# Two score tables of a two-block Swin kernel added up by VectorE inside its first two rounds, instead of by GpSimd and VectorE ahead of them

## The chip, the cores and the metric

The kernel runs on one core of one Trainium2 chip. The metric is the device time of one execution in microseconds (us); the median over repeated runs counts. The engines are TensorE (PE, with its weight loads as PEld), VectorE (DVE), ScalarE (ACT), GpSimd (POOL) and SyncE (SP). TensorE's clock has two levels, 1.2 and 2.4 GHz; the profile gives the granted clock as a share of the higher.

## The reference

Two Swin transformer blocks follow one another on x of shape (32, 56, 56, 96), in float32. Block 0 has 4 heads and a third layer norm inside its MLP, block 1 has 12 heads. In each block the image is shifted by 3 and cut into windows of 7 by 7 tokens:

```
h = roll(layer_norm(x), (-3, -3)) as windows of 49 tokens
q, k, v = h @ qkv_w + qkv_b
attn = softmax(q * scale @ k.T + rel_bias + attn_mask)
x = x + roll(attn @ v @ proj_w + proj_b, (3, 3))
m = gelu(layer_norm(x) @ fc1_w + fc1_b)      # block 0: then layer_norm(m)
x = x + m @ fc2_w + fc2_b
```

rel_bias is a table of relative positions that is the same for all windows; attn_mask is 0 or -100 and differs only between windows at the image's edge and the others. The sum of the two is a constant, in two forms: one for strips in the last row of windows and one for all others.

## The kernel before

The 32 images are cut into 256 strips of 8 windows (4 pairs of 98 tokens). A strip passes through a pipeline by hand: round i of the loop works on strip i (statistics of its first layer norm), strip i-1 (transposes), strip i-2 (attention of block 0), strip i-3 (its MLP), strip i-4 and i-5 (attention of block 1) and strip i-6 (its MLP, and the store). Each engine has its own `body(i)`, a list in fixed order of such steps; `iterate` writes out the first 9 rounds, loops over most of the rest and writes out the last ones. In rounds in which a strip doesn't exist the step is left out, so round 0 of VectorE is empty (the statistics of strip 0 were taken ahead), and round 1 holds two steps for it: `low_part_qk` of strip 0 and the statistics of strip 1. Engines wait for each other by semaphores that count upward.

The score of a window is not a matmul alone. Before the q k products are added up in a PSUM bank, ScalarE writes the sum of rel_bias and attn_mask there (`seed`, line 688, which reads the SBUF tensor `table`). The bank is then added to by TensorE (line 471). The first seeds are those of strip 0 in round 2.

`table` is 128 x 6272 in float32, two halves of 3136 columns: half 0 for ordinary strips, half 1 for the strips of the last row, of which the first is strip 224. ScalarE's DMA queue loads `t_in` (rel_bias; it is laid over the tensor `shifted`) and then the two masks into the halves of `table` (lines 619 and 621), three DMAs of 1568 KB each, and behind them, once VectorE has made them, two rows of biases into `wqkv` (line 624, 1.3 and 1.2 KB, semaphore `s_brow`). t_in is then added to each half:

- GpSimd adds half 0 as soon as t_in and mask 0 have landed (line 993).
- VectorE adds half 1 (line 982) at the end of its preparation, after the statistics of strip 0 (lines 846 to 854), and waits for GpSimd's half before its rounds begin.
- ScalarE waits for both (through `s_w` at 27 and `s_table`) before its first round, and so before its first table load (line 633).

VectorE's preparation is one chain in which every step waits for the one before: weights are scaled by the layer norms' gains (lines 810 to 815), split into a high and a low part (817 and 818 for the MLP; 831 and 832 for q and k, which wait for `s_brow` at 32), and the constant rows written (834). TensorE waits for `s_w` at 26 and for `s_brow` and then writes 6 of the 8 PSUM banks full once (line 401, 12 instructions). Its last instruction lets ScalarE go on (`s_wps` at 5), which then loads its function tables in turn: Gelu before that wait, then Exp, then Gelu (line 633). In round 1 GpSimd's normalised strip 0 (`rstdA` line 1000, `xnA` lines 1007 and 1011) is transposed by TensorE (line 407), and ScalarE reads the transpose out (`xqT_high` line 646, `xnT` line 647), after which TensorE makes v (line 450), k and q (422, 423, 425). SyncE's queue then spreads k over the heads (`kM`, line 342), and TensorE multiplies (line 471).

The code around the additions before:

```
            stats(Strip(0, 0), "A0", ahead=True)
            dve.wait_ge(s_tables[0], 32)
            dve.wait_ge(s_tables[1], 16)
            done(dve.tensor_tensor(table[:, NT:2 * NT], table[:, NT:2 * NT], t_in, ALU.add))
            dve.wait_ge(s_table, 1)
            iterate(dve, body)
```

Of the kernel before, what the change touches and what calls it, by code (L numbers as in the profile page):

```python
# [81 lines left out]
def swin_program(nc, d, out, ns=NSTRIP, last_row_from=NSTRIP - NSTRIP // ROWS_IN_IMAGE):  # L82
    f32, f32r = mybir.dt.float32, mybir.dt.float32r
    ALU, ACT, AX = mybir.AluOpType, mybir.ActivationFunctionType, mybir.AxisListType
    ctx = ExitStack()
    with ctx:
# [18 lines left out]
        NT = UNIT_COLS * NUNIT  # L105
        table = sb("table", [128, 2 * NT])
# [69 lines left out]
        s_tables = [sem(f"s_tables{v}") for v in (0, 1)]  # L176
# [77 lines left out]
        def bank_free(x, use):  # L254

            at = [n for n, _, _ in BANKS].index(use)
            own, wraps = BANKS[at][1], 0
            for _ in range(4 * len(BANKS)):
                at -= 1
                if at < 0:  # L260
                    at, wraps = at + len(BANKS), wraps + 1
                other, lag, bank = BANKS[at]
                y = Strip(x.i, x.off + lag + wraps - own)
                if bank == bank_of[use] and y.exists(ns):
                    semaphore, per, c = over[other]
                    return semaphore, y.count(per, c)
            return None
# [8 lines left out]
                      (rows[L][:, :], d[f"rows{L}"]), (wproj[L][:, :], d[f"wproj{L}"])]  # L276
        NCONST = 16 * len(loads)

        NMEMSET, NW_BROW, NW = 13 + len(O_BANKS), 4, 27

        def iterate(eng, body):

# [89 lines left out]
        def _(pe):  # L372
# [20 lines left out]
                          start=(c == 0), stop=False)  # L393
            pe.matmul(ps[5][0:PT, 0:C], ones[0:1, 0:PT], rows[0][0:1, W3[0]:W3[0] + C], start=False, stop=True)
            pe.matmul(ps[6][0:PT, 0:C], ones[0:1, 0:PT], rows[1][0:1, W3[1]:W3[1] + C], start=True, stop=True).then_inc(s_wps, 1)
            pe.wait_ge(s_w, NW - 1)
            pe.wait_ge(s_brow, 32)
            for n in range(8):
                if n in O_BANKS:
# [216 lines left out]
        def _(act):  # L616
# [7 lines left out]
                act.dma_start(wqkv[L][C:C + 1, :], brow[L][0:1, :]).then_inc(s_brow, 16)  # L624
            act.wait_ge(s_wps, 5)
            act.wait_ge(s_w, NW)
            act.wait_ge(s_table, 1)

            def table_ahead(x, n):

# [52 lines left out]
            def seed(x, L, u):  # L683

                if x.exists(ns):
                    if free_from := bank_free(x, f"sc{L}{u}"):
                        act.wait_ge(*free_from)
                    act.activation(ps[bank_of[f"sc{L}{u}"]][0:SP, 0:UNIT_COLS], table_of(x, L, u), ACT.Copy).then_inc(s_sd[L], 1)  # L688
# [84 lines left out]
        def _(dve):  # L773
# [16 lines left out]
            def done(ins, wait=True):  # L790
                step[0] += 1
                ins.then_inc(s_w, 1)
                if wait:
                    dve.wait_ge(s_w, step[0])
# [80 lines left out]
            def shift(x, L, u):  # L875
                if not x.exists(ns):
                    return
                dve.wait_ge(s_s[L], x.count(UNITS[L], u + 1))
                buf = unit_buffer(L, u)
                s = ps[bank_of[f"sc{L}{u}"]][0:SP, 0:UNIT_COLS].rearrange("p (h k) -> p h k", k=TOK)  # L880
                dve.tensor_reduce(negmax[:, buf, :], s, AX.X, ALU.max, negate=True).then_inc(s_mx[L], 1)  # L881
                if x.back().exists(ns):
                    dve.wait_ge(s_ex[L], x.back().count(UNITS[L], u + 1))
                dve.wait_ge(s_mx[L], x.count(UNITS[L], u + 1))
                dve.tensor_tensor(shifted[0:SP, buf, :].rearrange("p (h k) -> p h k", k=TOK), s,  # L885
                                  free(negmax[:, buf, 0:1], (1, 8), (0, TOK)), ALU.add).then_inc(s_sh[L], 1)
# [49 lines left out]
            def finish0(x):  # L936
# [11 lines left out]
                                                   op0=ALU.mult, op1=ALU.add)  # L948
                ins.then_inc(s_fin[0], 1)

            def body(i):
                s0, s1, s2, s3, s4, s5, s6 = Strip(i, 0), Strip(i, 1), Strip(i, 2), Strip(i, 3), Strip(i, 4), Strip(i, 5), Strip(i, 6)
                shift(s5, 1, 3)
                finish0(s4)
                normalise(s3, 0)
                stats(s4, "A1")
                shift(s5, 1, 4)
                shift(s5, 1, 5)
                residual(s3, 0)
                stats(s3, "M0")  # L960
                low_part(s6, 1)
                shift(s2, 0, 0)
                low_part_qk(s4, 1)
                shift(s2, 0, 1)
                normalise(s5, 1)
                low_part_qk(s1, 0)
                low_part(s3, 0)
                stats(s0, "A0")
                residual(s5, 1)
                stats(s5, "M1")  # L970
                finish1(s6)
                shift(s4, 1, 0)
                shift(s4, 1, 1)
                shift(s4, 1, 2)
                third_stats(s3)
# [1 line left out]


            stats(Strip(0, 0), "A0", ahead=True)
            dve.wait_ge(s_tables[0], 32)  # L980
            dve.wait_ge(s_tables[1], 16)
            done(dve.tensor_tensor(table[:, NT:2 * NT], table[:, NT:2 * NT], t_in, ALU.add))  # L982
            dve.wait_ge(s_table, 1)
            assert step[0] == NW
            iterate(dve, body)

        @block.gpsimd
        def _(pool):
            for L in (0, 1):
                pool.memset(kM[L][:, :, :], 0.0).then_inc(s_memset, 1)  # L990
                pool.memset(vM[L][:, :, :, :, :], 0.0).then_inc(s_memset, 1)
            pool.wait_ge(s_tables[0], 32)
            pool.tensor_tensor(table[:, 0:NT], table[:, 0:NT], t_in, ALU.add).then_inc(s_table, 1)

            def inverse_root(x, n):
                if x.exists(ns):
                    pool.wait_ge(s_var[n], x.count(1, 1))
                    if x.back().exists(ns):
                        pool.wait_ge(s_xn[n], x.back().count(1, 1))
                    pool.tensor_tensor(rstd[n][:, :], var_eps[n][:, :], minus_half[:, :], ALU.pow).then_inc(s_rstd[n], 1)  # L1000

            def norm(x, n):
                if not x.exists(ns):
                    return
                if x.back().exists(ns):
                    pool.wait_ge(s_xt[n], x.back().count(1, 1))
                pool.tensor_tensor(xn[n][:, :, :], SRC[n][:, :, :], free(mv[n][:, 0, 0:1], (2, PAIRS), (0, C)),
                                   ALU.subtract).then_inc(s_xc[n], 1)
                pool.wait_ge(s_xc[n], x.count(1, 1))
                pool.wait_ge(s_rstd[n], x.count(1, 1))  # L1010
                pool.tensor_tensor(xn[n][:, :, :], xn[n][:, :, :], free(rstd[n][:, 0:1], (1, PAIRS), (0, C)),
                                   ALU.mult).then_inc(s_xn[n], 1)

            def add_bias(x, L):
                if x.exists(ns):
                    pool.wait_ge(s_xo[L], x.count(1, 1))
                    if x.back().exists(ns):
                        pool.wait_ge(s_fin[L], x.back().count(1, 1))
                    pool.tensor_tensor(x_biased[L][:, :, :], x_mid[L][:, :, :], free(bfc2[L][:, 0:1], (0, PAIRS), (1, C)), ALU.add)\
                        .then_inc(s_xb[L], 1)  # L1020

            def squares(x):
                if not x.exists(ns):
                    return
                pool.wait_ge(s_ge[0], x.count(HCH, HCH))
                if x.back().exists(ns):
                    pool.wait_ge(s_f2[0], x.back().count(1, 1))
                pool.tensor_tensor(hid_sq[:, :, :], hid[0][:, :, :], hid[0][:, :, :], ALU.mult).then_inc(s_sq, 1)  # L1028
                pool.wait_ge(s_sq, x.count(3, 1))
                pool.tensor_tensor(hid_ss[:, :], hid_sq[:, 0, :], hid_sq[:, 1, :], ALU.add).then_inc(s_sq, 1)  # L1030
                pool.wait_ge(s_sq, x.count(3, 2))
                pool.tensor_tensor(hid_ss[:, :], hid_ss[:, :], hid_sq[:, 2, :], ALU.add).then_inc(s_sq, 1)

            def rstd_of_third(x):
                if x.exists(ns):
                    pool.wait_ge(s_v3, x.count(4, 4))
                    if x.back().exists(ns):
                        pool.wait_ge(s_fin[0], x.back().count(1, 1))
                    pool.tensor_tensor(rstd3[:, :], var3[:, :], minus_half[:, :], ALU.pow).then_inc(s_rstd3, 1)

            def body(i):
                s0, s3, s4, s5 = Strip(i, 0), Strip(i, 3), Strip(i, 4), Strip(i, 5)
                inverse_root(s4, "A1")
                norm(s4, "A1")
                inverse_root(s3, "M0")
                norm(s3, "M0")
                inverse_root(s0, "A0")
                add_bias(s3, 0)
                squares(s3)
                norm(s0, "A0")  # L1050
                inverse_root(s5, "M1")
                rstd_of_third(s3)
                norm(s5, "M1")
                add_bias(s5, 1)

            iterate(pool, body)
# [88 lines left out]
```

## Time and profile before

| | |
|---|---|
| median of 3 runs | 6497.58 us (6496.65 to 6502.27) |
| span of the profiled execution | 6496.8 us, 0.8 us under that median; no other time is given for it |
| TensorE busy | 6430.3 us (99%) |
| ScalarE busy | 5702.6 us (88%) |
| VectorE busy | 5350.0 us (82%) |
| GpSimd busy | 4516.1 us (70%) |
| granted TensorE clock, mean | 0.993 |

The span is the time from the first to the last instruction. "Busy" is the time in which an engine had an instruction under way, whether it computed or was held up in it. Because one strip passes per round, a few us at the beginning or the end stand once in the total, and a change in a round stands some 250 times in it.

### The profile page before, as it was taken

Reading aid. Unit: us, or ns where it says so; the run is one execution under the profiler, and the core shown is the slowest. Engines: PE = TensorE matmul, PEld = TensorE weight load, DVE = VectorE, ACT = ScalarE, POOL = GpSimd, SP = SyncE. Lnnn points to the kernel's source line nnn. Section 1 sums busy time; section 2 is a strip of 40 time slices with the busy share of each in tenths; the row PEclk is TensorE's granted clock in tenths of the full one; section 3 lists DMA queues with packets and bytes.
Section 4 is the critical chain, followed back from the end, with each engine's and each line's share of the span. In section 5 each row is a group of like instructions: output and inputs, shape, how many; then the busy total and the mean of one; then the engine's idle time right before and its main releaser. Section 6 shows DMA issues by size and latency. Waiting matters only on the chain.

```text
span 6496.8 us, 288677 instructions
## 1 busy us (share of the span) xinstructions
PE 6430.3 (99%) x97836; PEld 5929.2 (91%) x97836; DVE 5350.0 (82%) x19240; ACT 5702.6 (88%) x12312; POOL 4516.1 (70%) x4617
## 2 busy tenths in 40 slices
PE   6999999999999999999999999999999999999999
PEld 5999999999999999999999999999999999999998
DVE  5888888888888888888888888888888888888886
ACT  5888888888888888888888888888888888888887
POOL 4676767676767676777777777767676767676764
PEclk8999999999999999999999999999999999999998
DMA  2111111111111111111111111111111111111111
GB/s 68 51 51 50 51 50 51 50 50 50 51 50 51 50 52 49 52 49 51 50 50 50 50 51 50 51 50 51 49 51 50 51 50 51 50 50 50 51 50 36
DMA packets 604534, 327.88 MB, mean 50 GB/s; under 512 B 449916, under 2 KB 603902, under 8 KB 604094
## 3 DMA queue, kind: packets, MB, share of 16 engines
q1 hardware_dynamic: 603992, 322.32, 18.9%
q10 hardware_dynamic: 486, 4.82, 0.2%
q8 instruction: 35, 0.57, 0.0%
q14 instruction: 21, 0.17, 0.0%
HBM read 82.89 MB, written 38.54 MB: 19 GB/s over the span
## 4 chain that ended last, share of the span: by engine, by line
PE 98%; DVE 1%; issue 0%; ACT 0%; POOL 0%; DMA 0%; SPq 0%; DVEq 0%; ACTq 0%; POOLq 0%
PE ps L407 22%; PE ps L558 17%; PE ps L504 13%; PE ps L471 10%; PE ps L422 8%; PE ps L425 7%; PE ps L423 7%; PE ps L450 6%; PE ps L528 6%; PE ps L565 2%; PE ps L401 0%; DVE wfc_high L817 0%; DVE negmax L881 0%; DMA kM<-kT 0%; DMA wproj<-in_wproj 0%
## 5 line engine op out<-in xcount | busy, mean ns | idle before, releaser
L1000 POOL TENSOR_TENSOR rstdA<-var_epsA,minus_half 98x4 f32<-98x4 f32 x512 | 521.3, 1018 | 1348.7 <-DVE var_epsA L854 1348.6
L885 DVE TENSOR_TENSOR shifted<-ps,negmax 113x392 f32<-113x392 f32 x2048 | 1160.6, 567 | 241.7 <-DVE negmax L881 54.6
L881 DVE TENSOR_REDUCE negmax<-ps 113x8 f32<-113x392 f32 x2048 | 1144.6, 559 | 218.0 <-PE ps L471 217.9
L703 ACT ACTIVATE probsT<-ps 98x392 f32<-98x392 f32 x2048 | 959.4, 494 | 343.4 <-PE ps L407 342.8
L696 ACT ACTIVATE probs<-shifted 113x392 f32<-113x392 f32 x2048 | 1044.6, 522 | 125.2 <-DVE shifted L885 124.5
L407 PE MATMUL ps<-ident,probs 113*98 113x113 f32 x8192 | 1076.2, 264 | 9.5 <-ACT probs L696 8.1
L688 ACT ACTIVATE ps<-table 113x392 f32 (+1 forms) x2048 | 941.5, 499 | 28.4 <-DVE x_mid L908 2.4
L504 PEld LDWEIGHTS ps<-vM,probsT 98*49 98x49 f32 x32768 | 816.7, 125 | 137.7 <-issue 73.8
L504 PE MATMUL ps<-vM,probsT 98*49 98x18 f32 (+1 forms) x32768 | 899.6, 202 | 0.1
L407 PEld LDWEIGHTS ps<-ident,probs 113*98 113x98 f32 x8192 | 823.9, 130 | 47.9 <-ACT probs L696 12.5
L720 ACT ACTIVATE hid<-ps,bfc 128x392 f32<-128x392 f32 x1536 | 786.0, 586 | 14.8 <-PE ps L425 8.8
L1000 POOL TENSOR_TENSOR rstdM<-var_epsM,minus_half 98x4 f32<-98x4 f32 x512 | 518.2, 1012 | 386.5 <-DVE var_epsM L854 386.5
L633 ACT ACT_TABLE_LOAD x524 | 672.3, 1283 | 45.9 <-DVE table L982 36.8
L471 PE MATMUL ps<-kM,qT 32*49 32x196 f32 (+1 forms) x20480 | 688.1, 299 | 14.1 <-ACT ps L688 7.3
L558 PE MATMUL ps<-wfc,hid 128*98 128x97 f32 x6144 | 665.7, 255 | 0.0
L558 PEld LDWEIGHTS ps<-wfc,hid 128*98 128x98 f32 x6144 | 599.6, 168 | 0.0
L558 PE MATMUL ps<-par,hid 128*98 128x96 f32 (+1 forms) x6144 | 579.5, 251 | 0.7 <-ACT hid L720 0.7
L422 PE MATMUL ps<-xnT_high,wfc_high 96*128 96x392 f32 x1536 | 575.4, 375 | 2.9 <-DVE xnT_low L872 1.3
L471 PEld LDWEIGHTS ps<-kM,qT 32*49 32x49 f32 (+1 forms) x20480 | 438.5, 118 | 140.9 <-issue 98.1
L1028 POOL TENSOR_TENSOR hid_sq<-hid 128x1176 f32<-128x1176 f32 x256 | 549.1, 2145 | 14.8 <-ACT hid L720 14.8
L558 PEld LDWEIGHTS ps<-par,hid 128*98 128x98 f32 x6144 | 557.1, 168 | 1.2 <-ACT hid L720 1.2
L423 PE MATMUL ps<-xnT_high,wfc_low 96*128 96x392 f32 x1536 | 527.0, 343 | 0.0
(105 smaller groups left out, 15058.1 us busy)
## 6 DMA issues: line engine op xcount, KB each, us to landing
kM<-kT SPq DMA_DIRECT2D x512, 85.8 KB
vM<-vA SPq DMA_DIRECT2D x1024, 41.3 KB
vM<-vA SPq DMA_DIRECT2D x1024, 38.3 KB
x_in<-in_x SPq DMA_DIRECT2D x256, 147.0 KB
x_again<-in_x SPq DMA_DIRECT2D x256, 147.0 KB
kM<-kT SPq DMA_DIRECT2D x1024, 36.8 KB
x_keep<-x_next SPq DMA_DIRECT2D x256, 147.0 KB
out_y<-y_out SPq DMA_DIRECT2D x256, 147.0 KB
```

Of the source, the lines that this page charges most:

```text
L407: return pe.matmul(out, x, ident[0:rows, 0:rows], start=first, stop=last, is_transpose=True, skip_group_check=True)
L422: pe.matmul(out, w_high, x_high, start=True, stop=False)
L423: pe.matmul(out, w_low, x_high, start=False, stop=False)
L471: mm = pe.matmul(ps[bank_of[f"sc{L}{u}"]][HALF[h]:HALF[h] + TOK, n * p:n * (p + 1)], qT[L][r, t:t + TOK], kM[L][r, :, t:t + TOK], start=Fa ...
L504: mm = pe.matmul(g[HALF[h]:HALF[h] + TOK, col:col + width], probsT[:, unit_buffer(L, u), p * heads // 2 + n, h, :], vM[L][:, 2 * (first + ...
L558: mm = pe.matmul(g[0:PT, p * step:p * step + width], hid[L][:, c, t], w, start=(p == c == 0), stop=(c == HCH - 1), skip_group_check=True)
L688: act.activation(ps[bank_of[f"sc{L}{u}"]][0:SP, 0:UNIT_COLS], table_of(x, L, u), ACT.Copy).then_inc(s_sd[L], 1)
L696: act.activation(probs[:, buf, :], shifted[0:SP, buf, :], ACT.Exp).then_inc(s_ex[L], 1)
L703: act.activation(probsT[:, unit_buffer(L, u), :, :, :], free(ps[bank_of[f"T{L}{u}"]][0:PT, 0:1], (SP, 4), (64, 2), (1, TOK)), ACT.Copy).th ...
L881: dve.tensor_reduce(negmax[:, buf, :], s, AX.X, ALU.max, negate=True).then_inc(s_mx[L], 1)
L885: dve.tensor_tensor(shifted[0:SP, buf, :].rearrange("p (h k) -> p h k", k=TOK), s, free(negmax[:, buf, 0:1], (1, 8), (0, TOK)), ALU.add).t ...
L1000: pool.tensor_tensor(rstd[n][:, :], var_eps[n][:, :], minus_half[:, :], ALU.pow).then_inc(s_rstd[n], 1)
```

## The change

Both halves are now added by VectorE, in its `body`: half 0 as the first thing of round 0 and half 1 as the first thing of round 1 (`add_table`). GpSimd's addition is gone, as is VectorE's wait for it. ScalarE's wait for `s_table` before its first round is gone, and `s_w` ends at 26; a wait for `s_table` at 2 stands before each seed of strip 0 instead.

```
--- before.py
+++ after.py
@@ -276,7 +276,7 @@
                       (rows[L][:, :], d[f"rows{L}"]), (wproj[L][:, :], d[f"wproj{L}"])]
         NCONST = 16 * len(loads)
 
-        NMEMSET, NW_BROW, NW = 13 + len(O_BANKS), 4, 27
+        NMEMSET, NW_BROW, NW = 13 + len(O_BANKS), 4, 26
 
         def iterate(eng, body):
 
@@ -393,7 +393,7 @@
                           start=(c == 0), stop=False)
             pe.matmul(ps[5][0:PT, 0:C], ones[0:1, 0:PT], rows[0][0:1, W3[0]:W3[0] + C], start=False, stop=True)
             pe.matmul(ps[6][0:PT, 0:C], ones[0:1, 0:PT], rows[1][0:1, W3[1]:W3[1] + C], start=True, stop=True).then_inc(s_wps, 1)
-            pe.wait_ge(s_w, NW - 1)
+            pe.wait_ge(s_w, NW)
             pe.wait_ge(s_brow, 32)
             for n in range(8):
                 if n in O_BANKS:
@@ -624,7 +624,6 @@
                 act.dma_start(wqkv[L][C:C + 1, :], brow[L][0:1, :]).then_inc(s_brow, 16)
             act.wait_ge(s_wps, 5)
             act.wait_ge(s_w, NW)
-            act.wait_ge(s_table, 1)
 
             def table_ahead(x, n):
 
@@ -683,6 +682,8 @@
             def seed(x, L, u):
 
                 if x.exists(ns):
+                    if x.known and x.i == x.off:
+                        act.wait_ge(s_table, 2)
                     if free_from := bank_free(x, f"sc{L}{u}"):
                         act.wait_ge(*free_from)
                     act.activation(ps[bank_of[f"sc{L}{u}"]][0:SP, 0:UNIT_COLS], table_of(x, L, u), ACT.Copy).then_inc(s_sd[L], 1)
@@ -948,8 +949,16 @@
                                                    op0=ALU.mult, op1=ALU.add)
                 ins.then_inc(s_fin[0], 1)
 
+            def add_table(x, v):
+
+                if x.known and x.i == v:
+                    dve.wait_ge(s_tables[v], 32 - 16 * v)
+                    dve.tensor_tensor(table[:, v * NT:(v + 1) * NT], table[:, v * NT:(v + 1) * NT], t_in, ALU.add).then_inc(s_table, 1)
+
             def body(i):
                 s0, s1, s2, s3, s4, s5, s6 = Strip(i, 0), Strip(i, 1), Strip(i, 2), Strip(i, 3), Strip(i, 4), Strip(i, 5), Strip(i, 6)
+                add_table(s0, 0)
+                add_table(s0, 1)
                 shift(s5, 1, 3)
                 finish0(s4)
                 normalise(s3, 0)
@@ -977,10 +986,6 @@
 
 
             stats(Strip(0, 0), "A0", ahead=True)
-            dve.wait_ge(s_tables[0], 32)
-            dve.wait_ge(s_tables[1], 16)
-            done(dve.tensor_tensor(table[:, NT:2 * NT], table[:, NT:2 * NT], t_in, ALU.add))
-            dve.wait_ge(s_table, 1)
             assert step[0] == NW
             iterate(dve, body)
 
@@ -989,8 +994,6 @@
             for L in (0, 1):
                 pool.memset(kM[L][:, :, :], 0.0).then_inc(s_memset, 1)
                 pool.memset(vM[L][:, :, :, :, :], 0.0).then_inc(s_memset, 1)
-            pool.wait_ge(s_tables[0], 32)
-            pool.tensor_tensor(table[:, 0:NT], table[:, 0:NT], t_in, ALU.add).then_inc(s_table, 1)
 
             def inverse_root(x, n):
                 if x.exists(ns):
```

On VectorE, where its preparation ends and its rounds begin, before (`table<-table,shifted` is the addition of t_in to one half; `xqT_low` is the first step of round 1):

```order
L854 TENSOR_SCALAR var_epsA<-mvA 98x4 [waits s_bnA0]
L982 TENSOR_TENSOR table<-table,shifted 128x3136 [waits s_tables1,s_tables0]
L864 TENSOR_TENSOR xqT_low<-ps,xqT_high 96x392 [waits s_xeA0,s_table,s_w]
L846 BN_STATS bnA<-x_in 98x6 [waits s_xnA0,s_load]
L846 BN_STATS bnA<-x_in 98x6 x3
```

and with the change:

```order
L855 TENSOR_SCALAR var_epsA<-mvA 98x4 [waits s_bnA0]
L956 TENSOR_TENSOR table<-table,shifted 128x3136 [waits s_tables0]
L956 TENSOR_TENSOR table<-table,shifted 128x3136 [waits s_tables1]
L865 TENSOR_TENSOR xqT_low<-ps,xqT_high 96x392 [waits s_xeA0]
L847 BN_STATS bnA<-x_in 98x6 [waits s_xnA0,s_load]
L847 BN_STATS bnA<-x_in 98x6 x3
```

The two additions stand next to one another, since round 0 holds nothing else for VectorE, and ahead of the first step of round 1.

On GpSimd, from its last memset to its first strip, before:

```order
L991 MEMSET vM 98x864
L993 ISA
L993 TENSOR_TENSOR table<-table,shifted 128x3136 [waits s_tables0]
L1000 TENSOR_TENSOR rstdA<-var_epsA,minus_half 98x4 [waits s_varA0]
L1007 TENSOR_TENSOR xnA<-x_in,mvA 98x384
```

and with the change:

```order
L996 MEMSET vM 98x864
L1003 ISA
L1003 TENSOR_TENSOR rstdA<-var_epsA,minus_half 98x4 [waits s_varA0]
L1010 TENSOR_TENSOR xnA<-x_in,mvA 98x384
```

The addition is gone, and GpSimd's first arithmetic is that of strip 0. TensorE's and SyncE's instructions and waits are the same in both kernels; on ScalarE only the waits differ, at the first table load and at the eight seeds of strip 0.

## Rows read from the trace of the kernel before

**Rows 1.** The page, busy time of the engines and the chain by line.
```profile
PE 6430.3 (99%) x97836; PEld 5929.2 (91%) x97836; DVE 5350.0 (82%) x19240; ACT 5702.6 (88%) x12312; POOL 4516.1 (70%) x4617
...
PE 98%; DVE 1%; issue 0%; ACT 0%; POOL 0%; DMA 0%; SPq 0%; DVEq 0%; ACTq 0%; POOLq 0%
```

**Rows 2.** Groups by line, TensorE, 200 to 6400 us: count | busy, mean ns | idle before.
```profile
L471 PE MATMUL ps<-kM,qT 32*49 32x196 f32 (+1 forms) x19920 | 667.3, 298 | 3.9 <-ACT ps L688 0.2 <-DMA kM<-kT 0.2
```

**Rows 3.** The chain that ended last, 0 to 50 us: start, duration, what.
```profile
21.66 6.83 DVE wfc_high L817
...
32.03 7.34 PE ps L401 x12
...
42.42 0.20 ACT spark_gelu L633
```

**Rows 4.** Timeline, 0 to 60 us: start, duration, engine, line, operation [idle before].
```profile
20.68 0.35 DVE L817 CAST wfc_high<-wfc 96x384 fp32r<-96x384 f32 x1
...
21.43 6.83 POOL L993 TENSOR_TENSOR table<-table,shifted 128x3136 f32<-128x3136 f32 x1 [17.13 <-DMA table<-in_mask]
21.66 6.82 DVE L817 CAST wfc_high<-wfc 96x384 fp32r<-96x384 f32 x1
...
29.81 0.27 DVE L831 CAST wqk_high<-wqkv 97x224 fp32r<-97x224 f32 x1
```

**Rows 5.** Timeline, 0 to 40 us, ScalarE's DMA queue: start, duration of the issue.
```profile
16.97 2.16 ACTq L624 DMA_DIRECT2D wqkv<-brow  x2
```

**Rows 6.** The tile table, 0 to 60 us: mask DMAs, their first and last start, landing.
```profile
L621 ACTq DMA_DIRECT2D table<-in_mask x2: 450/452/453, 11.5 to 12.0; - x2
...
DMA to landing us min/median/max: 9.9/11.5/13.2
```

**Rows 7.** Windows: busy by engine, clock, DMA share, GB/s last.
```profile
24.00:24.50 0.50, 0.00 (x0) 0.00 (x0) 0.50 (x1) 0.00 (x0) 0.50 (x1) 1.00 0.20 55
24.50:25.00 0.50, 0.00 (x0) 0.00 (x0) 0.50 (x1) 0.00 (x0) 0.50 (x1) 1.00 0.01 1
```

**Rows 8.** Timeline, 32 to 60 us: strip 0 on its way to the first scores.
```profile
33.28 3.43 DVE L982 TENSOR_TENSOR table<-table,shifted 128x3136 f32<-128x3136 f32 x1
33.45 4.14 POOL L1000 TENSOR_TENSOR rstdA<-var_epsA,minus_half 98x4 f32<-98x4 f32 x1 [5.19 <-DVE var_epsA L854]
...
38.47 0.83 POOL L1011 TENSOR_TENSOR xnA<-xnA,rstdA 98x384 f32<-98x384 f32 x1
...
39.35 0.54 PE L407 MATMUL ps<-ident,xnA 98*96 98x98 f32 x4
...
42.53 0.47 ACT L646 ACTIVATE xqT_high<-ps 96x392 fp32r<-96x392 f32 x1
...
43.43 1.20 PE L450 MATMUL ps<-wqkv,xnT 97*98 97x100 f32 x8 [3.54 <-ACT xnT L647]
...
45.42 1.01 POOL L1000 TENSOR_TENSOR rstdA<-var_epsA,minus_half 98x4 f32<-98x4 f32 x1 [6.12 <-DVE var_epsA L854]
...
47.04 0.91 ACT L688 ACTIVATE ps<-table 113x392 f32<-113x392 f32 x2
...
49.53 1.56 PE L471 MATMUL ps<-kM,qT 48*49 48x98 f32 x32 [2.92 <-DMA kM<-kT]
...
59.24 1.65 PE L450 MATMUL ps<-wqkv,xnT 97*98 97x100 f32 x8
```

**Rows 9.** Windows in the filling of the pipeline: PE busy first, clock third from the end.
```profile
42.00:44.00 2.00, 0.57 (x6) 0.57 (x7) 0.49 (x2) 1.97 (x5) 0.00 (x0) 0.99 0.00 0
44.00:65.00 21.00, 13.94 (x113) 11.34 (x111) 6.10 (x29) 10.74 (x21) 5.26 (x6) 0.51 0.15 38
68.00:81.00 13.00, 8.21 (x37) 7.28 (x38) 3.90 (x16) 5.92 (x11) 9.12 (x9) 0.50 0.05 11
82.00:91.00 9.00, 6.18 (x88) 4.88 (x90) 5.40 (x31) 3.63 (x8) 4.25 (x5) 1.00 0.17 53
92.00:109.00 17.00, 13.43 (x78) 10.95 (x77) 7.68 (x23) 11.61 (x24) 8.79 (x9) 0.51 0.13 32
```

More of the change, by code:

```diff
@@ L277, in swin_program @@
         NCONST = 16 * len(loads)
-        NMEMSET, NW_BROW, NW = 13 + len(O_BANKS), 4, 27
+        NMEMSET, NW_BROW, NW = 13 + len(O_BANKS), 4, 26
         def iterate(eng, body):
@@ L395, in _ @@
             pe.matmul(ps[6][0:PT, 0:C], ones[0:1, 0:PT], rows[1][0:1, W3[1]:W3[1] + C], start=True, stop=True).then_inc(s_wps, 1)
-            pe.wait_ge(s_w, NW - 1)
+            pe.wait_ge(s_w, NW)
             pe.wait_ge(s_brow, 32)
@@ L626, in _ @@
             act.wait_ge(s_w, NW)
-            act.wait_ge(s_table, 1)
             def table_ahead(x, n):
@@ L685, in seed @@
                 if x.exists(ns):
+                    if x.known and x.i == x.off:
+                        act.wait_ge(s_table, 2)
                     if free_from := bank_free(x, f"sc{L}{u}"):
@@ L949, in finish0, with add_table @@
                 ins.then_inc(s_fin[0], 1)
+            def add_table(x, v):
+                if x.known and x.i == v:
+                    dve.wait_ge(s_tables[v], 32 - 16 * v)
+                    dve.tensor_tensor(table[:, v * NT:(v + 1) * NT], table[:, v * NT:(v + 1) * NT], t_in, ALU.add).then_inc(s_table, 1)
             def body(i):
                 s0, s1, s2, s3, s4, s5, s6 = Strip(i, 0), Strip(i, 1), Strip(i, 2), Strip(i, 3), Strip(i, 4), Strip(i, 5), Strip(i, 6)
+                add_table(s0, 0)
+                add_table(s0, 1)
                 shift(s5, 1, 3)
@@ L979, in _ @@
             stats(Strip(0, 0), "A0", ahead=True)
[L980 to L983, printed above, removed]
             assert step[0] == NW
@@ L991, in _ @@
                 pool.memset(vM[L][:, :, :, :, :], 0.0).then_inc(s_memset, 1)
-            pool.wait_ge(s_tables[0], 32)
-            pool.tensor_tensor(table[:, 0:NT], table[:, 0:NT], t_in, ALU.add).then_inc(s_table, 1)
             def inverse_root(x, n):
```

## The prediction

> **What bounds the kernel.** I read the page first: TensorE is busy for 99% of the span and holds 98% of the chain that ended last [rows 1]. The groups of TensorE's instructions between 200 and 6400 us, where the rounds are all alike, show that the only idle time before any of its matmuls is 3.9 us in all, at line 471 [rows 2]. A round there is TensorE's own work. The change touches nothing in those rounds and nothing in TensorE's list, so it can pay or cost only once, in the preparation and in the first rounds, ahead of about 110 us, the end of the last stretch at the lower clock [rows 9]. There I read the chain of waits for the order of causes, the timeline for what two engines did at the same moment, the tile table for the landing of its DMAs, and windows for the clock. About 0.2% of the time, 13.0 us, is what a measurement of this kernel can tell from no change; the whole preparation ends at some 40 us, so any gain has to be large in it to be seen.
>
> The chain of the first 50 us has one odd piece: VectorE's cast into `wfc_high`, 6.83 us long [rows 3]. The timeline has the same cast twice, with the same shape: 0.35 us for block 0, 6.82 us for block 1 [rows 4]. What differs is GpSimd: its addition to the table begins at 21.43 and ends at 28.26, the slow cast begins at 21.66 and ends at 28.48 [rows 4]. So the cast was held until 0.22 us after GpSimd's addition, and everything behind it on VectorE with it. Behind it lie the rest of the preparation, TensorE's 12 instructions of line 401 (32.03, 7.34 us), ScalarE's changes of table up to the last at 42.42 [rows 3], and strip 0.
>
> **What it removes.** The addition on GpSimd goes. The cast falls from 6.82 to the 0.35 us of its twin: **6.47 us** earlier on VectorE. The step after it that has a wait of its own is line 831, which started at 29.81 [rows 4] and would now be reached at 29.81 - 6.47 = 23.34.
>
> **What is late next.** Line 831 waits for the bias rows in `wqkv`. Before, it had no wait to show, so their landing is not in the trace and I bound it. They were issued from 16.97 to 19.13 [rows 5], on the queue that still carried the masks. The second mask was issued at 12.0 and took 13.2 us, so it landed at 25.2; the first landed at 11.5 + 9.9 = 21.4, which is when GpSimd began [rows 6]. The DMA engines moved 55 GB/s in 24.0 to 24.5 and 1 GB/s in 24.5 to 25.0 [rows 7], so the last of the small rows cannot have landed much before 24.6. From above only 29.81 bounds it, when VectorE passed. I take 25.2, the landing of the mask that moved next to it, as a copy behind 4.7 MB should come with or just after the last of these: that takes back 25.2 - 23.34 = **1.86 us**, leaving 4.61. The ends are 24.6 (0.6 us better) and about 27.0, two us after the last bytes (1.8 us worse).
>
> The Trainium skill ("DMA: Bandwidth & Descriptors", Queues, rings and completion order) says that completions are not in order per issuing engine, but that each DMA engine consumes its descriptors in ring order and its semaphore write comes after its earlier writes; by that the rows land about with the mask, never well before it, and an early 23.3 is out.
>
> **What it adds.** A second addition on VectorE: 3.43 us by the row of the first [rows 8]. VectorE itself has room. It was idle from 36.71, when its addition ended, until the transpose's low part, which waits for ScalarE's 42.53 [rows 8]. The seeds read `table` at 47.04 [rows 8], and the second half is done at 33.28 - 4.61 + 2 x 3.43 = 35.5, so ScalarE's new waits are free by over 7 us; if this cover went, each us of delay would stand once in the end. Both inputs have landed by then.
>
> Its cost lies on GpSimd. `rstdA` of strip 0 took 4.14 us where its twin of the next strip took 1.01, and it ended at 37.59, 0.88 us after VectorE's addition ended at 36.71 [rows 8]. So that addition held GpSimd. Now two stand back to back. Either `rstdA` waits for both, or it slips in between and the subtraction after it waits for the second; by both, `xnA` ends one addition later than it would: 39.30 - 4.61 + 3.43 = 38.12 (39.30 is the end of line 1011, 38.47 + 0.83 [rows 8]). TensorE's turn of it began at 39.35 and ended at 39.89, so it now ends at 38.71. ScalarE's changes of table are paced by line 401 alone and end 4.61 us earlier, ready for line 646 at 37.92 instead of 42.53. So ScalarE waits 38.72 - 37.92 = **0.80 us** for the turn: GpSimd's path, which had about 2.6 us of slack before, has become the longer one. Left: 3.81.
>
> The Trainium skill ("SBUF — State Buffer", Who interferes with whom) has a rule that speaks against this change: a VectorE operation with two inputs in SBUF locks out a GpSimd instruction that reads SBUF, whole instruction by whole instruction, and whoever came first holds the pair. The trace agrees (4.14 against 1.01 us). By the rule the sum keeps the 0.80; if the second addition held nobody, the sum would lose that term and be 0.8 us better.
>
> **The clock.** TensorE's granted clock was 0.99 of full in 42 to 44 us and 0.51 from 44 to 65 [rows 9], after it had stood idle for 3.54 us ahead of line 450 [rows 8]. In the changed kernel it is idle between line 401 and the turn as well, from 34.8 to 38.2, so I let the clock fall one step earlier: line 450's first group of 8, on the path, then takes the 1.65 us of the next strip's group at the lower clock instead of 1.20 [rows 8]: **0.45 us** back. Bounds: 0, and 0.8 if the turn is slow too.
>
> **Sum.** 6.47 - 1.86 - 0.80 - 0.45 = 3.36 us. Behind it, every step of the first rounds waits for another engine or for a DMA of its own round, so all move together. Taking away ScalarE's wait for the table is by itself worth nothing: the additions ended at 36.71, but line 401, which it waits for too, ended at 32.03 + 7.34 = 39.37 [rows 3, 8]. The span goes from 6496.8 to 6493.4. The runs' median stood 0.8 above that span; taken off the median the time is 6497.58 - 3.36 = **6494.2 us**.
>
> **Rivals.**
> 1. *Held less, landed earlier.* The bias rows are there at 23.3 and the second addition holds nobody: all 6.47 us arrive, 6491.1. For it: nothing shows their landing. Against: the queue's traffic up to 24.5 and the 4.14 us. Chance 0.07.
> 2. *The cast was not held by GpSimd's addition* but by something that stays (the mask's DMA ran beside it too). Then nothing is won, and the second addition pushes `xnA` from 39.30 to 42.73, the turn's end to 43.32, and line 646 from 42.53 to 43.35: slower by 0.8 us, 6498.4. It decides once GpSimd's path is more than 2.6 us late. Against: the cast outlasted the DMA traffic by 4 us and ended with GpSimd's addition to 0.22 us. Chance 0.05.
> 3. *The clock in the filling.* From 44 to 109 us it was at the lower level for most of the time, with 9 us at full in 82 to 91 [rows 9]. The levels change with TensorE's pauses, and these shift. If the 6.18 us of matmuls in that full stretch ran at half, up to 6.2 us would be lost: 6500.4. If those of 68 to 81 (8.21 us at 0.50) ran at full, up to 4.1 would be won: 6490.1. Chance 0.08 for each of the two. That before's three runs lie 5.6 us apart agrees with such shifts.
> 4. *A round of the steady part changes its length*, through another phase between the engines. It needs 0.05 us in each of some 250 rounds to be 13 us, 6507 or more. TensorE's 3.9 us of idle time leave nothing to win there, and its list is the same, so I give 0.02 to slower, 0.01 to faster by over 13 us.
>
> **How the numbers follow.** The forecast, its three us, has 0.69; the rivals 0.07, 0.05, 0.16 and 0.03. The range goes from 6489.0 (below the faster clock, and rival 1 with a part of it) to 6500.0 (rival 2, and most of the slower clock); it takes in both ends of the landing. Same, within 13.0 us: 0.69 + 0.07 + 0.05 + 0.16 = 0.97, less 0.01 for clock shifts that add up: 0.96. Faster by more 0.015, slower by more 0.025.
>
> **What would show it.** In the changed profile: the second cast into `wfc_high` at 0.35 us; an idle stretch on VectorE ahead of line 832 (831 before) of about 1.9 us, that ends on a DMA near 25.2; line 401's group at about 27.4; two additions of 3.43 us; `rstdA` at 7 us or more, or a subtraction of 4; the turn of strip 0 at 38.2; ScalarE's `xqT_high` at 38.7; the first scores at 46.2 instead of 49.53 [rows 8]; rounds of the same length. A cast still at 6.8 us, or a `rstdA` at 1 us, would prove a step wrong. A time outside 6489 to 6500 would mean that something outside the first 110 us moved.

## The result, and the profile after

The changed kernel took 6478.17 us (median of 6 runs, 6473.17 to 6479.65), the kernel before 6497.66 us beside it (6 runs, 6494.0 to 6502.27). The ratio is 0.9966, with a 95% interval of 0.9956 to 0.9977: about 19.5 us faster. I had forecast 6494.2, which is 3.4 us faster, and a range of 6489.0 to 6500.0; to anything faster by more than 13 us I had given a chance of 0.015. The size was out by a factor of six.

The page of the changed kernel; its chain is TensorE's to the same 98% as in [rows 1]:

```profile
PE 6411.6 (99%) x97836; PEld 5920.2 (91%) x97836; DVE 5350.8 (83%) x19241; ACT 5701.7 (88%) x12312; POOL 4511.3 (70%) x4616
...
PE 98%; DVE 0%; POOL 0%; issue 0%; DMA 0%; ACT 0%; SPq 0%; DVEq 0%; ACTq 0%; POOLq 0%
```

The start came out as forecast. The timeline of the changed kernel, 20 to 60 us (start, duration, engine, line, operation, idle before):

```profile
20.55 0.36 DVE L818 CAST wfc_high<-wfc 96x384 fp32r<-96x384 f32 x1
...
21.53 0.36 DVE L818 CAST wfc_high<-wfc 96x384 fp32r<-96x384 f32 x1
...
25.24 0.28 DVE L832 CAST wqk_high<-wqkv 97x224 fp32r<-97x224 f32 x1 [1.94 <-DMA wqkv<-brow]
...
28.73 6.75 DVE L956 TENSOR_TENSOR table<-table,shifted 128x3136 f32<-128x3136 f32 x2
28.90 7.47 POOL L1003 TENSOR_TENSOR rstdA<-var_epsA,minus_half 98x4 f32<-98x4 f32 x1 [24.59 <-DVE var_epsA L855]
...
38.13 0.62 PE L407 MATMUL ps<-ident,xnA 98*96 98x98 f32 x4 [3.79 <-POOL xnA L1014]
38.78 0.49 ACT L645 ACTIVATE xqT_high<-ps 96x392 fp32r<-96x392 f32 x1 [1.18 <-PE ps L407]
...
39.72 1.65 PE L450 MATMUL ps<-wqkv,xnT 97*98 97x100 f32 x8 [0.97 <-ACT xnT L646]
...
46.27 1.56 PE L471 MATMUL ps<-kM,qT 48*49 48x98 f32 x32 [2.92 <-DMA kM<-kT]
```

Set against [rows 4] and [rows 8]: both casts take 0.36 us, VectorE then stands for 1.94 us until the bias rows land, `rstdA` is held for both additions, and the first scores start at 46.27 instead of 49.53, 3.26 us earlier. The rest does not come from here.

It comes from the rounds. VectorE's last step of a strip, `y_out`, 205 rounds apart; of before, then of after:

```profile
1002.50 0.54 DVE L917 TENSOR_TENSOR y_out<-x_biased,ps 98x384 f32<-98x384 f32 x1
...
6110.34 0.54 DVE L917 TENSOR_TENSOR y_out<-x_biased,ps 98x384 f32<-98x384 f32 x1
```

```profile
1022.79 0.54 DVE L918 TENSOR_TENSOR y_out<-x_biased,ps 98x384 f32<-98x384 f32 x1
...
6114.89 0.54 DVE L918 TENSOR_TENSOR y_out<-x_biased,ps 98x384 f32<-98x384 f32 x1
```

That is (6110.34 - 1002.50) / 205 = 24.916 us a round before and (6114.89 - 1022.79) / 205 = 24.839 after, 0.077 us less. By this instruction the two profiled executions differ as follows (strip 3 is the fourth to be finished, strip 249 the 250th):

| | before | after | difference |
|---|---|---|---|
| first scores start | 49.53 | 46.27 | -3.26 |
| from there to y_out of strip 3 | 180.61 | 181.78 | +1.17 |
| to y_out of strip 249, 246 rounds | 6129.43 | 6110.67 | -18.76 |
| to the end | 137.21 | 132.74 | -4.47 |
| sum (span) | 6496.78 | 6471.46 | -25.32 |

The filling and the end vary with TensorE's granted clock: the last part of the table was between 129.4 us (e1, mean granted clock 0.93 in that stretch) and 138.1 us (e10, 0.84) in the profiles of the kernels below; before it was 137.2 at 0.84, after 132.7 at 0.89. The profiled execution of the changed kernel (6473.27 us) was the second shortest of its six.

**Where in the round.** I laid a round of each over the other, from `y_out` at 3045.63 before and at 3034.74 after. Every instruction of every engine up to 12.2 us into the round stands at the same place to 0.015 us, but for three of VectorE that start 0.12 us earlier and move nobody else. Then ScalarE's seeds of block 0 (line 688 before, 689 after) start 0.09 us earlier, with them TensorE's scores of block 0 (0.07 to 0.08 us), and everything behind. Before:

```profile
3057.65 0.55 DVE L908 TENSOR_TENSOR x_mid<-x_again,ps 98x384 f32<-98x384 f32 x1
3057.84 0.53 ACT L696 ACTIVATE probs<-shifted 113x392 f32<-113x392 f32 x1 [0.23 <-DVE shifted L885]
...
3058.46 0.92 ACT L688 ACTIVATE ps<-table 113x392 f32 x2
...
3059.00 0.50 PE L407 MATMUL ps<-ident,xnA 98*96 98x98 f32 x4
...
3059.52 0.89 PE L471 MATMUL ps<-kM,qT 48*49 48x98 f32 x32
```

and after:

```profile
3046.75 0.54 DVE L909 TENSOR_TENSOR x_mid<-x_again,ps 98x384 f32<-98x384 f32 x1
3046.95 0.53 ACT L697 ACTIVATE probs<-shifted 113x392 f32<-113x392 f32 x1 [0.23 <-DVE shifted L886]
...
3047.48 0.92 ACT L689 ACTIVATE ps<-table 113x392 f32 x2
...
3048.10 0.50 PE L407 MATMUL ps<-ident,xnA 98*96 98x98 f32 x4
...
3048.55 0.89 PE L471 MATMUL ps<-kM,qT 48*49 48x98 f32 x32
```

From the start of `x_mid` to that of the seeds it is 0.81 us before and 0.73 after; from the turn (line 407) to the scores 0.52 and 0.45. The turn lasts 0.50 in both, so before the scores hardly wait by the profile (0.02 us), and after they overlap the turn's end by 0.05: together the 0.07 us. (The ends of matmuls in the profile are modelled, so how the 0.07 splits up rests on that model; the starts don't.)

The trace also holds ScalarE's register and semaphore instructions, which the views leave out. Between `x_mid` and the seed stands one register operation, which works out the seed's column in `table` and carries the wait for the bank that `x_mid` frees. From its start to the seed's start:

```
                  median   min     max    (245 rounds)
before            0.232    0.231   0.241
after             0.153    0.153   0.154
```

In the changed kernel a gap of 0.09 us stands 7 instructions earlier instead, behind an exponential (0.103 against 0.014 us to the next record). And the waits that the change put at strip 0's seeds have made ScalarE's list ahead of the loop 7 instructions longer (417 in place of 410; `s_table` once less, eight times more). Waits are instructions of the list where they don't fit on the one behind them; one semaphore instruction carries up to two (in e8 below 80 waits make the list 40 longer). The loop itself is the same 109 instructions. VectorE has such a gap too, of 0.12 us. Its list ahead of the loop is one instruction shorter, and the gap moved from ahead of one instruction to behind it; e2 below has it at the new place as well, and the long rounds.

### The profile page after: what moved, and what is told of

Same layout as the page of the kernel before. It is cut to its first block, busy times and chain, and to the rows that moved or that the text cites. A ratio compares the mean times of both kernels' runs of the same rounds, so it can differ in the third digit from the quotient of the medians.

```text
span 6471.5 us, 288682 instructions
## 1 busy us (share of the span) xinstructions
PE 6411.6 (99%) x97836; PEld 5920.2 (91%) x97836; DVE 5350.8 (83%) x19241; ACT 5701.7 (88%) x12312; POOL 4511.3 (70%) x4616
## 4 chain that ended last, share of the span: by engine, by line
PE 98%; DVE 0%; POOL 0%; issue 0%; DMA 0%; ACT 0%; SPq 0%; DVEq 0%; ACTq 0%; POOLq 0%
PE ps L407 22%; PE ps L558 17%; PE ps L504 13%; PE ps L471 10%; PE ps L422 8%; PE ps L425 7%; PE ps L423 7%; PE ps L450 6%; PE ps L528 6%; PE ps L565 2%; POOL rstdA L1003 0%; DMA wqkv<-brow 0%; DMA kM<-kT 0%; DMA wproj<-in_wproj 0%; DVE negmax L882 0%
## 5 line engine op out<-in xcount | busy, mean ns | idle before, releaser
L697 ACT ACTIVATE probs<-shifted 113x392 f32<-113x392 f32 x2048 | 1044.5, 522 | 126.8 <-DVE shifted L886 126.7
L425 PE MATMUL ps<-xnT_low,wfc_high 96*128 96x392 f32 x1536 | 526.6, 343 | 0.0
```

The source lines that it names most:

```text
L425: return pe.matmul(out, w_high, x_low, start=False, stop=True)
L697: act.activation(probs[:, buf, :], shifted[0:SP, buf, :], ACT.Exp).then_inc(s_ex[L], 1)
```

## The experiments

Three theories were open at first. A: a gap of about 0.08 us lies at a fixed place of ScalarE's list, so in each round of the loop ahead of whatever instruction sits there, and the change moved it off the seed. B: the earlier start put the engines into another phase. C: the list of VectorE or GpSimd decides, not ScalarE's. All kernels below were timed in turns with the kernel before, and each difference is to its median beside them.

**Waits alone (e1).** The kernel before, with the eight waits and nothing else:

```
-            act.wait_ge(s_table, 1)            # ahead of ScalarE's rounds
+                    if x.known and x.i == x.off:
+                        act.wait_ge(s_table, 1)    # in seed()
```

> The kernel before with one thing changed: ScalarE waits for the table (s_table at 1) at each of the eight seeds of strip 0 instead of once ahead of its rounds. No addition is moved. Its list ahead of the loop grows by 7 instructions, as in the change. Theory A (the place in ScalarE's list decides: a gap of about 0.08 us in its issue falls once per round at a fixed place of the list, in the kernel before right on the first seed of block 0): rounds of 24.84 us instead of 24.916, and no gain at the start, so 6497.7 - 245 x 0.077 = 6479, give or take 4. Theory B (the earlier start brings the engines into another, better phase): rounds stay at 24.916 and the time at 6497.7, since the start is not earlier. Theory C (GpSimd's or VectorE's list decides): also 6497.7.

6476.67 us against 6498.42, ratio 0.9965 (0.9951 to 0.998). The first scores start at 49.26, as in before, so nothing is won at the start; the register operation is 0.153 us ahead of the seed, the round 24.833 us (on ScalarE, from one return of the loop to the next). Waits that are met long before bring the whole gain of the change: 21.8 us here, against 19.5 and, with e7 below, 19.3 for the change.

**The change with the list as long as before (e2).**

```
-                    if x.known and x.i == x.off:
-                        act.wait_ge(s_table, 2)    # in seed()
+                    if L == 0 and x.known and x.i == x.off:
+                        act.wait_ge(s_table, 2)    # ahead of the copy xnT, in turned()
```

> The changed kernel with one wait for the table instead of eight, at ScalarE's copy xnT of strip 0 (line 646), an instruction that had no wait. VectorE's and GpSimd's lists are those of the change, both additions as there; ScalarE's list ahead of the loop is as long as before (410 in place of 417). Theory A: the first scores still at 46.3 us, rounds of 24.916 us again, 6497.7 - 3.4 = 6494.3, which is what I had forecast for the change. Theory B and C: rounds of 24.84 and the changed kernel's 6478.

6495.68 against 6498.42, ratio 0.9994 (0.9985 to 1.0004): 2.7 us less, within what the measurement can tell from nothing. The first scores start at 46.27 and the round is 24.918 us, the register operation 0.232 us ahead of the seed. B falls with these two kernels: one has the early start and the long round, the other the late start and the short round. Theory C, that VectorE's or GpSimd's list decides, falls as well: these are not what differs, since they are those of the change in e2 and those of before in e1. The windows 1000 to 1200 us of e1, then of e2 (length, busy of PE, PEld, DVE, ACT, POOL, clock, DMA share, GB/s):

```profile
1000.00:1200.00 200.00, 200.00 (x3073) 185.23 (x3072) 167.96 (x603) 178.25 (x386) 142.18 (x146) 1.00 0.20 51
```

```profile
1000.00:1200.00 200.00, 199.88 (x3065) 184.84 (x3064) 167.15 (x602) 177.86 (x385) 141.42 (x146) 1.00 0.19 50
```

**The gap moved in small steps (e3, e4, e9, e10).** Each is the kernel before with ScalarE's list ahead of the loop longer by 1, 3 and 2 instructions, or shorter by 1:

```
             act.wait_ge(s_table, 1)
+            for _ in range(2):                 # e3; 5 in e4, 3 in e9
+                act.wait_ge(s_table, 1)
```

```
-                        act.wait_ge(s_k[L], x.back().count(1, 1))      # e10, in turned()
+                        if not x.known or x.i > 2:
+                            act.wait_ge(s_k[L], x.back().count(1, 1))
```

> The kernel before with ScalarE's list ahead of the loop one instruction longer (two more waits for the table, met already, behind the one that is there). Theory A: the gap falls one instruction earlier in the round, ahead of the register operations of the first seed (line 688). These sit directly ahead of it on the same engine, so the seed is late by the same 0.08 us: rounds of 24.91, 6497.7. B and C: 6497.7 as well; this run tells only with the next one.

> The kernel before with ScalarE's list ahead of the loop three instructions longer (five more waits for the table, met already). Theory A: the gap falls behind line 651 and ahead of the exponential's register operation, where ScalarE has to wait 0.6 us for VectorE in each round anyway: it is hidden, rounds of 24.84, 6479 give or take 4. B and C: 6497.7.

> The kernel before with ScalarE's list ahead of the loop two instructions longer (three more waits for the table, met already). The gap now falls directly ahead of the exponential (line 696), behind the register operation that waits 0.6 us for VectorE in each round. If the gap is a fetch that goes on while the sequencer waits, it is hidden there: rounds of 24.83, 21 us under before. If each gap delays the instruction behind it whatever the sequencer did, the exponential and the seed behind it are 0.08 us late: rounds of 24.91, no gain.

> The kernel before with ScalarE's list ahead of the loop one instruction shorter (in round 2 the wait for the k of the strip before is left out where the transpose is read; the wait for its q covers it, which TensorE makes later). The gap falls behind the first seed of block 0 instead of ahead of it, where ScalarE is still busy with that seed for 0.4 us. If only the place between the seed's register operation and the seed costs: rounds of 24.83 and 21 us under before. If the second seed's place costs as well: rounds of 24.9.

| kernel | list ahead of the loop | the gap shows up | round, us | median, us | before beside it | ratio (95%) |
|---|---|---|---|---|---|---|
| before | 410 | between register operation and seed, 0.079 | 24.916 | | | |
| e10 | 409 | behind the seed, 0.081 | 24.833 | 6475.72 | 6493.49 | 0.9975 (0.9965 to 0.9985) |
| e3 | 411 | nowhere | 24.833 | 6475.47 | 6498.42 | 0.9964 (0.995 to 0.9978) |
| e9 | 412 | ahead of the exponential, 0.078 | 24.834 | 6475.96 | 6493.49 | 0.9974 (0.9964 to 0.9983) |
| e4 | 413 | nowhere | 24.833 | 6475.75 | 6498.42 | 0.9965 (0.9951 to 0.9979) |
| e1 | 417 | 7 earlier | 24.833 | 6476.67 | 6498.42 | 0.9965 (0.9951 to 0.998) |

Of all these places one costs. e3 was a miss of mine: I had taken ScalarE's own work for what the seed waits for, so that a gap ahead of the register operation should cost the same. It does not, because the register operation waits for `x_mid` in each round, and the gap passes in that wait; e4's lies in another wait. In these two the gap itself can't be seen, only that the seed's 0.079 us are gone. In e9 the gap is not hidden, as half of what I wrote there supposed: the exponential does start 0.078 us later; but the register operation behind it still starts on `x_mid`, and the seed with it.

**One more instruction ahead of the seed (e6).**

```
+                    if not x.known and (L, u) == (0, 0):
+                        act.wait_ge(s_w, NW)
+                        act.wait_ge(s_w, NW)
                     act.activation(...)            # in seed()
```

> The changed kernel with one more semaphore instruction on ScalarE, met already, directly ahead of the first seed of block 0 in every round of the loop. Theory A (the start of this seed sets TensorE's scores and with them the round): the sequencer reaches the seed 0.04 to 0.08 us later, and the round grows by as much: 24.88 to 24.91 us, 6487 to 6498. If the seed were not on the path: 24.84, 6478.

6472.47 against 6493.43, ratio 0.9971 (0.9959 to 0.9982), round 24.834 us: no cost, the same error as in e3. The instruction was placed ahead of the register operation, not between it and the seed as meant, and ran 0.025 us behind the exponential's start; the register operation followed 0.355 us later, when `x_mid` was ready.

**Blocks of 256 (e8, e11, e12).** The changed kernel with 40, 249 and 269 instructions more ahead of the loop, made of waits that are met already:

```
+            for _ in range(80):                # 498 in e11, 538 in e12
+                act.wait_ge(s_w, NW_BROW)
             act.wait_ge(s_wps, 5)
```

> The changed kernel with ScalarE's list ahead of the loop 40 instructions longer again (47 more than before; 80 waits that are met already, at a place where ScalarE waits for TensorE anyway). Theory A: the gap moves to a place some 11 instructions before the loop's first, so at the back end of the round, near the seeds of block 1 or the exponentials; unless one of these decides for TensorE, the round stays at 24.84, and the time at 6478. A round of 24.9 would mean that there is a second place that costs.

> The changed kernel with ScalarE's list ahead of the loop 249 instructions longer (498 waits that are met already): 256 more than before. If the gap comes wherever the list passes from one block of 256 instructions to the next, it is back ahead of the first seed of block 0: register operation to seed 0.232 us, rounds of 24.916 us, and the time within 6 us of before's (the waits themselves take 249 x 0.077 = 19.2 us of ScalarE's 15.2 us of idle time ahead of its first round, so the start is later by some 4 us). If the gap in before came from something else, such as the sum of waits ahead of the loop: 0.153 us, rounds of 24.83, 16 us under before.

> The same with 20 instructions more (276 more than before), as the control for the cost of so many waits. With blocks of 256 the gap falls 20 instructions earlier in the round than in the kernel before: register operation to seed 0.153 us, rounds of 24.83 to 24.84 us, about 18 us less than the kernel with 256, though it starts 1.5 us later.

| kernel | list | register operation to seed | round, us | median, us | before beside it | ratio (95%) |
|---|---|---|---|---|---|---|
| e8 | 457 | 0.153 | 24.834 | 6476.12 | 6493.43 | 0.9971 (0.9959 to 0.9982) |
| e11 | 666 = 410 + 256 | 0.253 | 24.939 | 6503.8 | 6499.89 | 1.0006 (0.9996 to 1.0016) |
| e12 | 686 | 0.153 | 24.837 | 6478.27 | 6499.89 | 0.9962 (0.9948 to 0.9977) |

The gap returns ahead of the same instruction when the list is 256 longer, and 20 instructions further it is gone from there again. The time of e11 also holds a later start (first scores at 51.06 us, in e12 at 52.36), since that many waits outlast ScalarE's idle time; the rounds are free of that. e12 carries more of the added waits than e11 and is still 25.5 us faster. e11's gap is 0.100 us (0.253 - 0.153) where before's is 0.079, and its rounds are 0.106 us longer than the short ones (24.833) where before's are 0.083: the round pays the gap in full. TensorE shows it in the windows, e11 first, e12 second:

```profile
1000.00:1200.00 200.00, 199.69 (x3061) 184.60 (x3060) 167.19 (x602) 178.16 (x387) 140.83 (x144) 1.00 0.19 50
```

```profile
1000.00:1200.00 200.00, 200.00 (x3067) 185.15 (x3066) 167.96 (x604) 178.92 (x389) 140.69 (x144) 1.00 0.19 50
```

e8 adds one thing: there the loop's return on ScalarE takes 0.155 us to the next record, in all the others of the first table 0.245 (0.255 in e11 and e12), and no gap is left inside the loop. I had expected the gap at the back end of the round; it left the loop. By the distance of 256 e8's 109 instructions lie in one block, those of the others in two. The slower return costs no time here: e8's rounds are as long as e3's or e10's, because ScalarE waits right behind it (1.72 us in the others, 1.81 in e8).

**Is it a refill by DMA in each round?** No. The DMA packets of before of the kind "instruction", in the whole execution:

```profile
q8 instruction: 35, 0.57, 0.0%
q14 instruction: 21, 0.17, 0.0%
```

and between 240 and 6300 us, where the loop runs, there is none in before and none in e11; these are all the queues of that stretch, before first:

```profile
q1 hardware_dynamic: 572872, 305.48, 19.2%
```

```profile
q1 hardware_dynamic: 572508, 305.00, 19.3%
```

So the gap comes in each round though nothing is fetched from outside. What ScalarE does in it the runs don't show.

**The second addition later (e5).** The changed kernel, with half 1 added at the end of round 1:

```
                 add_table(s0, 0)
-                add_table(s0, 1)
...
                 stats(s0, "A0")
+                add_table(s0, 1)
...
-                        act.wait_ge(s_table, 2)
+                        act.wait_ge(s_table, 1 + L)
```

> The changed kernel with the addition of half 1 moved behind the statistics of strip 1, still in round 1, so that only one addition stands ahead of strip 0's path on GpSimd; the seeds of block 0 wait for half 0 alone, those of block 1 for both. The instructions ahead of the loop are as many as in the change. If the second addition holds GpSimd (the 0.80 us of my sum): rstdA of strip 0 takes about 4.1 instead of 7.47 us, xnA ends near 34.7, the turn is no longer what ScalarE waits for, and the first scores start at 45.1 to 45.4 instead of 46.27; rstdA of strip 1 is held instead, within the slack it has. Time about 1 us under the changed kernel's, which the runs cannot tell. If it holds nobody: no row moves.

> The changed kernel itself once more, beside the others of this call: 6478, rounds of 24.84 us.

6472.74 against 6493.43, ratio 0.9967 (0.9956 to 0.9978); the changed kernel once more (e7) 6474.16 beside it, 0.9969 (0.9958 to 0.9981), with rounds of 24.836 us, so the two are not told apart by time. In the timeline of e5 the hold that my sum had at 0.80 us is seen:

```profile
29.14 4.13 POOL L1003 TENSOR_TENSOR rstdA<-var_epsA,minus_half 98x4 f32<-98x4 f32 x1 [24.84 <-DVE var_epsA L855]
...
35.03 0.54 PE L407 MATMUL ps<-ident,xnA 98*96 98x98 f32 x4
...
41.14 4.12 POOL L1003 TENSOR_TENSOR rstdA<-var_epsA,minus_half 98x4 f32<-98x4 f32 x1 [6.16 <-DVE var_epsA L855]
...
45.23 1.56 PE L471 MATMUL ps<-kM,qT 48*49 48x98 f32 x32 [2.91 <-DMA kM<-kT]
```

`rstdA` of strip 0 is held for one addition, that of strip 1 for the other, and the first scores start at 45.23, in e7 at 46.01 and in the changed kernel's first profile at 46.27. By its trace the start is 0.8 to 1.0 us ahead of the change.

## Why the prediction was wrong

**Right, by its own steps.** The cast fell from 6.82 to 0.36 us (forecast 0.35). The wait for the bias rows was 1.94 us and ended at 25.24 (forecast 1.86 and 25.2). `rstdA` took 7.47 us (forecast 7 or more), so the second addition held GpSimd too. The turn began at 38.13 (38.2), ScalarE's `xqT_high` at 38.78 (38.7), line 450 took 1.65 us (1.65), and the first scores came 3.26 us earlier (3.36). An agreement to 0.1 us is luck: where the additions are early the first scores start between 48.44 and 49.53 us (before, e1, e3, e4, e9, e10), with the change's between 45.76 and 46.27 (after, e2, e6, e7). e2, which is the change without the moved gap, took 6495.68, 2.7 us under its before, where the sum said 3.36; that fits, but an interval that takes in 1 does not show it, and e1, without the early start, gained no less than the change. The early start is shown by the traces alone. Rivals 1 and 2 did not happen. The Trainium skill's rule on the port pair ("SBUF — State Buffer", Who interferes with whom) agrees with every one of the held instructions: 7.47 us beside two additions, 4.13 and 4.12 beside one each, 1.01 beside none.

**Wrong: "The change touches nothing in those rounds".** It touched none of the instructions in them, but it moved ScalarE's loop by 7 places in its list. That is worth 18.76 us over 246 rounds in the profiles (0.076 to 0.077 each), nearly all of the 19.5. My part on ScalarE said that only its waits differ, and priced them as waits; their number was not counted, nor what they do to the place of the code behind them. Rival 4 had a changed round, but by another phase between the engines, which e1 and e2 rule out. That the round became shorter is luck: the kernel before happened to have its gap at the one place that costs, and e11, the same change with a longer list, is no faster than before.

**Wrong: "A round there is TensorE's own work" and "TensorE's 3.9 us of idle time leave nothing to win there"** (the ground for giving rival 4 a chance of 0.01 on the fast side). ScalarE's seed set a part of the round: 0.079 us less ahead of it gave 0.083 us in each. The 3.9 us of [rows 2] were the sign, not the size. They stood at line 471 alone, in nearly all rounds (0.016 us each), while no other group of matmuls showed a wait. The same rows for TensorE's weight loads and matmuls at line 471, 200 to 6400 us, of before:

```profile
L471 PEld LDWEIGHTS ps<-kM,qT 32*49 32x49 f32 (+1 forms) x19920 | 425.3, 118 | 126.7 <-issue 85.6
```

and of after:

```profile
L471 PEld LDWEIGHTS ps<-kM,qT 32*49 32x49 f32 (+1 forms) x19968 | 422.5, 118 | 113.5 <-issue 39.8
...
L471 PE MATMUL ps<-kM,qT 32*49 32x196 f32 (+1 forms) x19968 | 669.1, 298 | 0.4 <-DMA kM<-kT 0.4
```

The matmuls' wait goes from 3.9 to 0.4 us, and the rounds give back five times that; the idle time ahead of the weight loads, which falls from 126.7 to 113.5 us, is the nearer sign. In the rounds shown above the scores that were ready overlapped the turn by 0.05 us; coming 0.07 us late they lost that overlap first, and only the last 0.02 were shown as idle. So TensorE's 99.9% (199.88 of 200 us, the same in before and e2) was not a bound, and a wait of hundredths in each round stood for 0.08.

**The clock** changed its pattern in the filling, as rival 3 held possible, but for 1.2 us (the second line of the table); at the end the profiles of different kernels lie up to 8.7 us apart (129.4 to 138.1), with the granted clock at 0.93 and 0.84.

What stays open: what ScalarE does in the gap, why it is 0.079 us in the kernel before and 0.100 in e11, whether the 0.12 us on VectorE have the same cause, and where the limits of the blocks lie in the lists of the other engines. One distance of 256 was run, and none of 512.

## What to carry to other kernels

Where one engine is full, its rounds can still be set by a chain of hundredths from another engine: compare start to start over many rounds, and take a small wait that recurs at one line of a "full" engine as a lost overlap that may be several times its size. A change ahead of a loop moves the loop's place in the engine's list; count the instructions it adds there, waits too, and when a loop's round changes without a change in it, pad the list by a few instructions and look again before the gain or loss is put down to what the change was meant to do. A comparison of two versions of a kernel with a long loop is worth no more than this effect, here 0.3%, unless the place is held still.

## What the runs showed of the hardware that I had not expected

- On ScalarE a gap of 0.08 to 0.10 us comes at a fixed place of the list, in every one of 245 rounds. With two more instructions ahead it fell two earlier in the round (e9), with seven more seven earlier (e1), with one less one later (e10). It came back at the same instruction when 256 were added, not when 276 were. A loop that lies across such a place has the gap once a round, and its return takes 0.09 to 0.10 us more (0.245 to 0.255 against 0.155), which cost nothing here.
- The Trainium skill ("Runtime: NRT & Kernel Launch", Instruction fetch mechanics) says that the instruction memory is refilled in blocks of 256 instructions, and that crossing a boundary costs "one DMA tail-bump, mostly hidden". The runs agree with the 256, but not with a refill as the cause of this gap, since no instruction packet moves in these rounds. Whether the gap is hidden depends on the place: free in all the kernels above that have it elsewhere, but 246 x 0.083 = 20 us where the instruction behind the gap is on the path.
- The register operation that waits for `x_mid` in each round covered what stood ahead of it on ScalarE: gap and added instruction cost nothing there (e3, e6), and the gap cost 0.083 us a round one instruction later.
